# Full attention's head sums with the queries as rows, their divisor as a ninth column, and weight pieces given the time they land

## What is computed

```python
x = x + 0.5 * ffn(layernorm(x))      # two layers: local attention (8 heads of 64), then a gated MLP
x = x + attn(layernorm(x))           # causal attention over all 256 tokens, 16 heads of 8
x = x + 0.5 * ffn(layernorm(x))
```

```python
scores = einsum('bhqd,bhkd->bhqk', q, k) / sqrt(8)          # q, k, v: x @ W + b, 16 heads of 8
weights = softmax(where(causal, scores, -inf), axis=-1)
out = einsum('bhqk,bhkd->bhqd', weights, v)                 # then heads side by side
return out @ Wo + bo
```

## Time and profile before

| | us |
|---|---|
| median of 3 runs (lowest, highest) | 1858.02 (1854.99, 1860.14) |
| the profiled execution, its own time | 1866.13 |
| its span, first to last instruction | 1864.3 |

### The profile page before, as it was taken

One profiled execution on the slowest core, in us unless ns is written; L12 is line 12 of the kernel. 1 busy time (PEld: TensorE's weight loads), 2 busy tenths in 40 slices (PEclk: granted clock), 3 DMA queues, 4 the chain that ended last, 5 costly groups with the idle time before them and its releaser, 6 DMA issues.

```text
span 1864.3 us, 51559 instructions
## 1 busy us (share of the span) xinstructions
PE 1680.3 (90%) x18560; PEld 1367.5 (73%) x18560; DVE 1479.3 (79%) x2938; ACT 1564.8 (84%) x4956; POOL 1286.7 (69%) x1528
## 2 busy tenths in 40 slices
PE   2798899989999999998988899899999999989987
PEld 2577778778877777777777677777687777777776
DVE  5788888688788687888889788876778775788886
ACT  1588799888999898998788888799999887988886
POOL 4899974487394657759998999920559570589991
PEclk9799999999999999999999999999999997999999
DMA  4101000000010000010100011000000000001000
GB/s 113 35 10 24 13 10 11 10 18 19 2 27 11 10 20 14 19 31 18 38 25 24 19 24 28 10 2 2 18 11 19 10 18 1 19 19 28 20 16 15
DMA packets 31701, 36.48 MB, mean 20 GB/s; under 512 B 7986, under 2 KB 18652, under 8 KB 31452
## 3 DMA queue, kind: packets, MB, share of 16 engines
q1 hardware_dynamic: 31452, 33.19, 7.4%
HBM read 5.91 MB, written 2.10 MB: 4 GB/s over the span
## 4 chain that ended last, share of the span: by engine, by line
POOL 37%; PE 23%; DVE 15%; ACT 15%; issue 9%; SPq 1%; DMA 0%; POOLq 0%; ACTq 0%; DVEq 0%
POOL rnorm L1031 13%; POOL parts L1021 11%; POOL parts L1035 8%; ACT probs L1090 8%; PE bank L1427 6%; PE bank L1510 4%; DVE parts L1358 4%; PE bank L1586 3%; POOL sums_floor L1028 3%; ACT turned L1108 2%; POOL rstd L1009 2%; DVE neg_max L1264 2%; PE bank L1546 2%; DVE sums L1365 2%; PE bank L1627 1%
## 5 line engine op out<-in xcount | busy, mean ns | idle before, releaser
L1090 ACT ACTIVATE probs<-bank,neg_max 128x128 f32<-128x128 f32 (+1 forms) x1536 | 584.7, 446 | 36.5 <-DVE neg_max L1264 35.5
L1021 POOL TENSOR_TENSOR parts<-parts 128x256 f32<-128x256 f32 x512 | 377.4, 763 | 161.8 <-DVE parts L1358 160.9
L1031 POOL TENSOR_TENSOR rnorm<-sums_floor,neg_half 128x8 f32<-128x8 f32 x256 | 431.9, 1687 | 21.3
L1090 ACT ACTIVATION_READ_ACCUMULATOR probs<-bank,neg_max 128x1 f32 x1536 | 401.5, 268 | 0.0
L1358 DVE TENSOR_TENSOR parts<-bank,rope 128x1024 f32<-128x1024 f32 x256 | 308.8, 1215 | 51.0 <-ACT squares L1137 49.7
L1264 DVE TENSOR_REDUCE neg_max<-bank 128x4 f32<-128x512 f32 (+1 forms) x448 | 287.5, 681 | 73.5 <-PE bank L1479 39.8
L1035 POOL TENSOR_TENSOR parts<-parts,rnorm 128x512 f32<-128x512 f32 x256 | 278.7, 1089 | 37.6 <-POOL rnorm L1031 1.3
L1510 PE MATMUL bank<-ident,probs 128*128 128x128 f32 x1792 | 253.5, 283 | 39.9 <-DVE probs L1279 19.4
L1108 ACT ACTIVATE turned<-bank 128x512 f32<-128x512 f32 x448 | 258.3, 661 | 34.1 <-PE bank L1510 33.5
L1510 PEld LDWEIGHTS bank<-ident,probs 128*128 128x128 f32 x1792 | 205.4, 145 | 78.3 <-issue 33.3
L1007 POOL TENSOR_SCALAR var_eps<-mean_var 128x2 f32<-128x2 f32 x112 | 32.3, 289 | 318.6 <-DVE mean_var L1297 313.6
(11 more groups left out here) (119 smaller groups left out, 3873.4 us busy)
## 6 DMA issues: line engine op xcount, KB each, us to landing
between<-val SPq DMA_DIRECT2D x192, 128.0 KB, 2.3
x_sb<-in_L_attn_x_dram SPq DMA_DIRECT2D x16, 128.0 KB, 2.7
out_dram<-x_sb SPq DMA_DIRECT2D x16, 128.0 KB, 1.9
raw_qkv<-in_L_ffn_wqkv_dram SPq DMA_DIRECT2D x2, 768.0 KB, 5.5
raw_w<-in_L_ffn_w_dram SPq DMA_DIRECT2D x2, 341.0 KB, 4.3
wo<-in_L_ffn_wo_dram SPq DMA_DIRECT2D x2, 256.0 KB
rope<-in_rope_dram SPq DMA_DIRECT2D x1, 256.0 KB, 3.0
w<-in_L_ffn_w_dram SPq DMA_DIRECT2D x2, 128.0 KB
```

What stands on the lines that cost most here:

```text
L1021: last = nc.gpsimd.tensor_tensor(joined[:, :, dst], joined[:, :, dst], sines[:, :, src], ALU.add)
L1031: nc.gpsimd.tensor_tensor(rnorm[:, u], sums_floor[:, u], neg_half[:], ALU.pow).then_inc(sems["pool_step"], 1)
L1090: last = nc.scalar.activation(probs[:, u, block:block + wide].rearrange("p b j -> p (b j)"), bank[:, at:at + P * wide], ACT.Exp, bias=neg_ ...
```

## The change

In full attention the turned probabilities become the stationary operand and the values the moving one, so the sums come out with queries as rows. The values are kept as [keys, head, 9], with a constant 1 in the ninth column, so the ninth column of the result is the sum of the row's probabilities. VectorE takes the reciprocal of it and multiplies. The heads of a sequence are transposed at the end by a new step OT, and the output projection is one matmul. The `accum_out` of the exponentials is left out in full attention, and so are the step N, the spread of the reciprocals and its copy. VALF has 128 columns in place of 512; the weights of v are not spread. The output weights and the bias of v are each loaded by one DMA. COME gets entries for two more pieces of weights and for the first layer norm. The planner's costs, due times and the order that follows from them are other ones throughout.

```diff
-                    i = INVERSE_OF[unit]
-                    pe.wait_ge(sems["inverse_ready"], count("inverse_ready", unit))
-                    for t in range(TILES):
-                        for h in range(UNIT):
-                            at, row = PAD_D * h, UNIT * t + h
-                            nc.tensor.matmul(bank[at:at + PAD_D, T + P * t:T + P * (t + 1)],
-                                             prob_inv[:, i, row:row + 1].to_broadcast([P, PAD_D]), ident[:],
-                                             start=True, stop=True)
-                    for t in range(TILES):
-                        for h in range(UNIT):
-                            at, of = PAD_D * h, 3 * P * h + T * t
-                            last = nc.tensor.matmul(bank[at:at + PAD_D, P * t:T], val[a][:, t, PAD_D * (UNIT * m + h):PAD_D * (UNIT * m + h + 1)],
-                                                    turned[:, u, of:of + T - P * t], start=(t == 0), stop=(t == TILES - 1),
+                    for h in range(UNIT):
+                        for n, (t, keys) in enumerate(((0, 0), (1, 0), (1, 1))):
+                            at, of = (FULL_D + 1) * (UNIT * t + h), P * (3 * h + n)
+                            last = nc.tensor.matmul(bank[:, at:at + FULL_D + 1], turned[:, u, of:of + P],
+                                                    valf[a][:, keys, UNIT * m + h], start=(keys == 0), stop=(keys == t),
                                                     skip_group_check=True)
...
+                if kind == "OT":
+                    for t in range(TILES):
+                        last = nc.tensor.transpose(bank[:, P * t:P * (t + 1)], o_full[set_of(step)][:, t], ident[:])
+                if kind == "WOF":
+                    last = nc.tensor.matmul(bank[:, 0:T], wof[:], y_t[s], start=True, stop=True)
...
-                    last = split_matmul(bank[:], hi[:, tok], lo[:, tok], wf_hi[:, 2], wf_lo[:, 2], True)
+                    last = split_matmul(bank[:, 0:C], hi[:, tok], lo[:, tok], wv_hi[:, 0], wv_lo[:, 0], True)
...
-                dve.wait_ge(sems["inverse_copied"], count("inverse_copied", step))
-                nc.vector.tensor_tensor(o_full[set_of(step)][:, m], bank[:, 0:T], inverse[:], ALU.mult).then_inc(sems["heads_scaled"], 1)
+                dve.wait_ge(sems["heads_summed"], count("heads_summed", step))
+                nc.vector.reciprocal(inv, heads[:, :, :, FULL_D:FULL_D + 1]).then_inc(sems["vector_step"], 1)
+                dve.wait_ge(sems["vector_step"], count("vector_step", step))
...
+                nc.vector.tensor_tensor(o_full[set_of(step)][:, :, cols].rearrange("p t (h d) -> p t h d", d=FULL_D),
+                                        heads[:, :, :, 0:FULL_D],
+                                        inv.to_broadcast([P, TILES, UNIT, FULL_D]),
+                                        ALU.mult).then_inc(sems["heads_scaled"], 1)
...
-                    last = nc.scalar.activation(probs[:, u, block:block + wide].rearrange("p b j -> p (b j)"),
-                                                bank[:, at:at + P * wide], ACT.Exp, bias=neg_max[:, u, row:row + 1],
-                                                accum_out=prob_sum[:, u, row:row + 1])
+                    dst = probs[:, u, block:block + wide].rearrange("p b j -> p (b j)")
+                    if is_full(ph):
+                        last = nc.scalar.activation(dst, bank[:, at:at + P * wide], ACT.Exp, bias=neg_max[:, u, row:row + 1])
...
+                if kind == "OT":
+                    nc.scalar.activation(y_t[s], bank[:, 0:T], ACT.Copy).then_inc(sems["heads_turned"], 1)
+                if kind == "VALF":
+                    nc.scalar.activation(valf[set_of(step)][:, n, :, 0:FULL_D],
+                                         bank[:, 0:C].rearrange("p (h d) -> p h d", d=FULL_D),
+                                         ACT.Copy).then_inc(sems["values_ready"], 1)
...
-COME = {("READY", 0, 0): 10.0, ("READY", 2, 0): 9.0, ("READY", 6, 0): 19.0, ("READY", 12, 0): 19.0,
-        ("READY", 21, 0): 37.0, ("FOLD", 0, 0): 13.0, ("FOLD", 1, 0): 13.0, ("FOLD", 2, 0): 37.0, ("FOLD", 0, 1): 23.0}
+COME = {("LNX", 0, 0): 8.5, ("READY", 0, 0): 10.0, ("READY", 2, 0): 9.0, ("READY", 6, 0): 19.5, ("READY", 12, 0): 19.5, ("READY", 15, 0): 19.5, ("READY", 18, 0): 19.5,
+        ("READY", 20, 0): 35.0, ("FOLD", 0, 0): 14.0, ("FOLD", 1, 0): 14.0, ("FOLD", 2, 0): 35.0, ("FOLD", 0, 1): 23.0}
...
-        return [(PE, 1.08), (ACTE, 0.28), (DVE, 0.34)] if is_full(ph) else [(PE, 0.97), (ACTE, 0.5)]
+        return [(PE, 1.5), (DVE, 0.4)] if is_full(ph) else [(PE, 0.97), (ACTE, 0.5)]
```

More of the change, by code:

```diff
@@ L286, in weights_of @@
         return [("FOLD", 0, 0, DENSE_LAYER[PHASES[ph][1]])]
-    if kind in ("QF", "VALF") and part == 0:
-        m = n // 2 if kind == "QF" else 2
-        return made(("wf_hi", m), ("wf_lo", m))
+    if kind == "QF" and part == 0:
+        return made(("wf_hi", n // 2), ("wf_lo", n // 2))
+    if kind == "VALF" and part == 0:
+        return made(("wv_hi", 0), ("wv_lo", 0))
     if kind == "QF" and part == 1:
-        return made(("biases", 0))
+        return made(("biases", 0), ("table", LAYERS - 1))
     if kind == "WOF":
@@ L361, in needs @@
                     wait(x, 1, x, 0)
-                    wait(unit, 0, x)
+                    if not is_full(ph):
+                        wait(unit, 0, x)
                 for x in turned_for(unit):
@@ L367, in needs @@
                     wait(sums_of(unit), 0, x)
-                if is_full(ph):
-                    wait(sums_of(unit), 0, unit)
                 for part in range(1, len(passes(sums_of(unit)))):
@@ L404, in lay_out @@
 def lay_out(after, due, patience):
-    pool, probs, turned, ropes, squares, high, hidden, sets, inverses, wide, splits = places = [Places(n) for n in (
-        POOL_BANKS, UNITS_KEPT, TURNED_KEPT, ROPES, SQUARES, 1, 1, SETS, INVERSES, 1, SPLITS)]
+    pool, probs, turned, ropes, squares, high, hidden, sets, splits = places = [Places(n) for n in (
+        POOL_BANKS, UNITS_KEPT, TURNED_KEPT, ROPES, SQUARES, 1, 1, SETS, SPLITS)]
     waiting, missing, then = [[] for _ in range(4)], {}, {}
@@ L466, in takes @@
             if before is not None:
-                for z in [(y, 1) for y in exps_of(before)] if part == 0 else [(y, 0) for y in turned_for(before)] + [(before, 0)]:
+                for z in [(y, 1) for y in exps_of(before)] if part == 0 else [(y, 0) for y in turned_for(before)]:
                     if z not in done:
@@ L738, in first_needed @@
     return out
+SCALED = [x for x, part in DVE_ORDER if x[0] == "N" or x[0] == "V"]
+INVERSE_OF = {x: n % 2 for n, x in enumerate(SCALED)}
 PE_NEEDS, ACT_NEEDS, DVE_NEEDS = (first_needed(order) for order in (PE_ORDER, ACT_ORDER, DVE_ORDER))
@@ L827, in macaron @@
         between = per_stream("between", [P, TILES, INNER], F32, range(SETS))
+        valf = per_stream("valf", [P, TILES, FULL_HEADS, FULL_D + 1], F32, range(SETS))
         o_t = q_t
-        o_full = [x[:].rearrange("p t (c q) -> p (t c) q", q=T) for x in between]
+        o_full = [x[:, 0, 0:TILES * C].rearrange("p (t c) -> p t c", t=TILES) for x in between]
         x_sb, state, normal, y_t, bn, mean_var, var_eps, rstd = (
@@ L1077, in exp_scores @@
                     act.wait_ge(sems["probs_turned"], later("probs_turned", turned_for(before)))
-                    if is_full(before[2]):
-                        act.wait_ge(sems["inverse_ready"], count("inverse_ready", before))
                 if not is_full(ph):
@@ L1571, in dense @@
                 if kind == "FOLD" and n == LAYERS:
-                    pe.wait_ge(f_loaded, 16 * N_FLOADS)
-                    for c in range(CHUNKS):
-                        last = nc.tensor.matmul(bank[:, 0:1], wof[:, c], biasf[:, 2, c:c + 1],
-                                                start=(c == 0), stop=(c == CHUNKS - 1))
+                    pe.wait_ge(b_loaded, 16 * N_BLOADS)
+                    last = nc.tensor.matmul(bank[:, 0:1], wof[:], bv[:], start=True, stop=True)
                 elif kind == "FOLD":
```

182 lines of the change are left out of this document (89 added, 93 removed), and 48 rows, old and new, of tables (DUE, LATER).

## The result

The change makes the kernel slower: 1997.9 us (median of 4 runs, 1989.57 to 2006.56) against 1857.83 us for the kernel before on the same chip, a ratio of 1.0755 [1.0699, 1.0811]. The forecast was 1876 us with a range up to 1922. The side was right, the size was not: +140 us where +18 were forecast. The profiled execution took 2006.56 us.

The account below looks back on a forecast made before the run. TensorE, with ScalarE close behind, was taken to bound the full-attention stretches. TensorE +58, idle time given back -25 and start -15 make +18 on the median of 1858: 1876 us, range up to 1922 (1825 to 1922).

Parts of the forecast that it names:

- TensorE, the sums over values: Full attention's sums: 24 records at 0.108 us make 2.60 us a unit, 1.38 more than before, +88 us.
- ScalarE: Accumulator reads -46, copy of the spread -17, VALF's copy -10, OT's copy +4: -69 us in sum.
- gave back 25: Full attention: ScalarE's relief shortens waits within TensorE's 62 us of idle time; 25 us taken off, ends 0 and 62.
- The start: First sequence no longer waits behind late weight pieces; TensorE gets it near 14 us, 16 earlier: -15 us, ends 0 and -19.
- TensorE, the rest: Shorter output projection -21.6, OT's two added transposes +3.5, VALF's narrower passes -11.5 us.
- VectorE: Reciprocal and product in full attention: same total taken, within 0.25 us a unit or 16 us, hidden by TensorE and ScalarE.
- A: Rival: ScalarE was the limit in full attention, so its 69 us and the start's 15 go: 1774 us; chance 0.06.
- C: Rival: TensorE's idle time covers all 58 us added, and 15 + 15 are gained: 1828 us; chance 0.18.
- B: Rival: 128-column weight loads hide behind one another, a unit's sums take 0.72 us: 1783 us; chance 0.08.
- E: Rival: start doesn't move, 1891 us; sign: first projection after 25 us; chance only given jointly with the forecast, 0.52.
- D: Rival: VectorE waits on sums longer than planned, 1911 to 1946 us; sign: over 30 us before the reciprocal; chance 0.16.

Follow-up runs that it names:

- half the loads: Changed kernel widened to 128 moving columns, with turned probabilities and values of full attention as fp32r, one weight load a matmul instead of two: 1826.15 us, ratio 0.9822.
- the kernel with 128 columns: Changed kernel in its own order, with 128 moving columns in place of 9 in full attention's sums, excess overwritten: 1894.89 us, ratio 1.0164.

## Why the prediction was wrong, step by step

The runs part the +140 us into three pieces. All but the form of the sums: 1826.81 - 1858 = -31. The form with the clock kept up: 1894.89 - 1826.81 = +68, both on one chip. The clock: 1997.9 - 1894.9 = +103. By the ratios the first is -37 and the last +110; so much play is in them.

- **TensorE, the sums over values: the step that failed.** It took a record's distance from the earlier trace rows, 0.108 us, and multiplied. The distance was right (0.110 measured). What failed is the reading of the price as the whole cost: that one column and 128 take the same time was taken to mean that they are the same to the chip. They aren't: with the thin ones the mean clock was 0.916, with 128 columns 0.979, and the low stretches took in work that nobody edited (0.53 from 609 to 612.5 us). The forecast even noted that the matmuls of one column in the earlier trace rows ran "while the clock is on its way up", and the earlier trace rows had the clock of each stretch; I never made a term of it. The term was worth +103 to +110 us, more than the forecast's whole sum, and none of the rivals held it.
- **The same step with the clock kept up** was forecast at +88 on TensorE and came at that: 64 x (2.63 - 1.22) = 90. Of it 68 reached the time in the new order and 65 (1923.02 - 1858) in the old one. TensorE's recorded busy time rose by 77.5 us in the new order (1641.1 to 1718.7), and its idle time fell by some 10.
- **ScalarE.** Its busy time fell by 62.6 us against 69 forecast, and 1024 accumulator reads are left. I gave back 25 of it. Measured, the accumulators alone, 45 us of ScalarE, cost 28 to 34, of which some 14 may be the clock's. So the size of the relief held. Whether 25 was too low a share depends on that part of the clock, and stays open.
- **The start.** The first transposes are at 13.84 us, as forecast (near 14). This was 16 us earlier, but the worth was put at -15, and alone it is 7 in the old order and 8 to 13 in the new one. I take it that TensorE starts earlier and then waits for work that other engines owe; no run shows it. The timeline of PE after:

```profile
13.84 0.66 PE L1623 MATMUL bank<-ident,normal 128*128 128x128 f32 x2 [13.84 <-DVE normal L1340]
```

- **TensorE, the rest.** WOF, VALF and OT were put at -30. TensorE's work shrank by about that: with the old form of the sums it is busy for 1641.1 us against 1680.3 before, 39 us less, of which the clock explains some 10 (84 us at the lower level instead of 104). But the forecast without the sums was 18 - 88 = -70, and -31 to -37 was measured. TensorE's idle time is the same, 1823.9 - 1641.1 = 183 us against 184, though ScalarE was relieved and the start came earlier. What those two bring by themselves, 28 and 8 us or more, doesn't add to the rest in this order; why stays open.
- **VectorE.** The steps as forecast cost nothing; its work changed by 3 us (1479.27 to 1476.3).

Had the clock held, the time would have been near 1895 (1888 by the ratio), inside the range and 12 to 19 us above the forecast.

Of the rivals, A (1774) and C (1828) are refuted by 1895 even at a steady clock, and B by the 0.110 us a record. E's sign did not show. D had the right side and its sign came, 159.3 us of wait where 30 were asked for, and its reason, sums longer than planned, was there too: the wait fell to 108 us with the clock kept up and to 36 us with half the loads, in the same order. But a third of the 159 went with the clock, which D did not have, and the form cost 68 us in the new order and 65 in the old one, both laid out for shorter sums, which doesn't part the wait from TensorE's own work. How much of the 68 us is this wait, and what an order made for sums of 2.6 us would save, is open; the one try at such an order was 79 us slower, with due times that were not set for it.

The Trainium skill, Perfetto Trace Analysis, section Identifying the Most-Contended Engine, names the share of weight loads as a better measure of TensorE than its matmul busy time. It rose from 73% to 78%, which points at TensorE; but it is 77% in the kernel with 128 columns, which is 103 us faster. Of the measures in the page's rows it is the granted clock that tells these two apart.

## What to carry to other kernels

Behind a load of 128 columns of weights a matmul took the same time with 9 moving columns as with 128 (0.108 and 0.110 us a record), but the kernel did not keep the same clock (0.916 and 0.979). Where many thin ones follow one another, price the clock's fall over all of TensorE's work around them, and read the clock's row of the page before any busy time. Widening the moving operand into neighbouring data took the fall away here without a longer record, and some 80 us at the lower level remained. An order laid out by a planner belongs to the cost table that its due times were chosen with; here a better cost alone made it 79 us worse, some 33 of which may be the clock's.

## What the chip showed that was not expected

- TensorE's clock fell to 0.53 in a window in which it was busy for 3.50 of 3.50 us. By moving columns of the sums (9, 32, 64, 128) the mean clock was 0.916, 0.947, 0.973, 0.979.
- The lower clock nearly doubles the distance of the sums' own records: 0.108 us at a granted clock of 1.00, about 0.2 at 0.50, with 9 moving columns and a load of 128.
- An edit of ScalarE alone changes TensorE's clock: with the accumulators back it fell from 0.916 to 0.904 with 9 columns and from 0.979 to 0.972 with 128, and the edit cost 41 and 28 us. Why wasn't looked into.
- VectorE's reciprocal of 128x256 took 1.75 us, against 0.207 of 128x8: an estimate of 1.546 / 248, some 6 ns, for each further element of a row.
